# One completion count per copy for the token scatters of a routed layer on one core

## The chip, the cores and the metric

The kernel runs on one core of one Trainium2 chip. The metric is the device time of one execution in microseconds (us), the median of the runs given. The engines named below are PE (TensorE), DVE (VectorE), ACT (ScalarE), POOL (GpSimd) and SP (SyncE, which here issues DMAs only).

## The reference

The program computes two transformer-like layers on 16 sequences of 256 tokens with 128 features (4096 tokens). Layer 0 is a small state-space mixer and a mixture of 8 experts with 2 chosen per token. Layer 1 is a 16-head attention with relative positions and a second mixture of experts with hidden size 512. The change touches only that last part, which the reference writes densely:

```python
logits = relu(xf @ Wr1 + br1) @ Wr2 + br2
gates = softmax(logits); tg, ti = top_k(gates, 2); tg = softmax(tg / 2)
out = silu(xf @ Ws1 + bs1) @ Ws2 + bs2              # shared expert, all tokens
for e in range(8):
    h = silu(xf @ We1[e] + be1[e]) @ We2[e] + be2[e]
    w = sum(tg * (ti == e), axis=-1)
    out = out + w[:, None] * h
```

## The kernel before, in words

The kernel does not compute every expert for every token. It copies each token's feature row twice, once for each chosen expert, into a DRAM table `dispatched_rows` (`xsD` in the code) that has an area of 4096 rows for each expert. It then works through 39 tiles (`NG`) of 256 rows, each belonging to one expert, and scatters the results back to `expert_results` (`yD`).

**Routing.** Tokens are handled in 8 chunks of 512 (`NC`), and two chunks form one of 4 groups (`GROUPS`). A group holds 8 columns of 128 tokens (`GN` is 8). For group g, DVE chooses the two experts (`choose(g)`, L1392), PE forms prefix sums (`ranks(g)`, L1906), and DVE turns them into row numbers (`destinations(g)`, L1414). The last instruction for each copy k (0 or 1) is the cast at L1424, which adds 1 to the semaphore `s_dest`. The feature rows themselves lie in `ROWS[0]` and `ROWS[1]`.

**Scattering, the place of the change.** POOL runs the loop at L725 to L735. For each group g and each copy k it waits for `s_dest`, then issues 8 indirect DMAs (L733), one for each column of 128 tokens, 129 floats per row. Ahead of each eight, the first one excepted, it waits at L730 until all earlier scatters have landed: all DMAs add 16 to the one semaphore `s_disp`, and the value waited for is 16 times the number issued so far. In all there are 4 x 2 x 8 = 64 scatters. The eights are called g0k0, g0k1, g1k0 and so on to g3k1 below. Nothing else runs on POOL between the first of them and the first result scatter of the tiles (L741).

**Who waits for the scatters.** SP does, once. After the tables of tiles are ready it loads the weights of the first four tiles (`load_weights`, L602), then waits at L613 for `s_sdn` to reach 8 (PE has finished the shared expert for all 8 chunks, which frees memory that the tiles use), then at L614 for all 64 scatters, and then loads the rows of the first four tiles (`load_rows`: a register load at L595 and the DMA at L596).

**What PE and DVE do meanwhile.** PE runs the shared expert: `shared_up(c)` (L1930) and `shared_down(c)` (L1940), whose last matmul adds 1 to `s_sdn`. For each chunk DVE waits for that count, adds a bias (L1428), multiplies by a gate (L1027) and adds to the residual (L1030), which adds 1 to `s_res`. The orders of `shared_up`, `shared_down`, `project` and `ranks` on PE and of `shared_out`, `choose` and `destinations` on DVE are written out by hand. PE waits for `s_res` to reach 8 at L2026, and then for the rows of tile 0 (L1999); its first instruction of the tiles is the transpose at L2002. Then each tile goes through L2002, L2011 (up), L925 (ACT), L2021 (down), L1518 (DVE) and L741 (POOL).

Of the kernel before, what the change touches and what calls it, by code (L numbers as in the profile page):

```python
# [26 lines left out]
NT = TOK // P  # L27
# [39 lines left out]
GN = GC * TPC  # L67
# [6 lines left out]
def build(nc, A, out):  # L74
    ctx = ExitStack()
    with ctx:
# [3 lines left out]
        def sem(name):  # L80
            return ctx.enter_context(nc.semaphore(name))
# [169 lines left out]
        ROWS = [v.rearrange("p (t n) -> p t n", t=NT) for v in (rows0, R.take(NT * RW))]  # L251
# [117 lines left out]
        s_tot = sem("s_tot")  # L369
        s_rank = sem("s_rank")  # L370
        s_dest = sem("s_dest")
        s_disp = sem("s_disp")
        s_sup = sem("s_sup")
        s_sact = sem("s_sact")
        s_sdn = sem("s_sdn")
# [44 lines left out]
        def _(sp):  # L420
# [71 lines left out]
            for c in range(NC):  # L492
# [3 lines left out]
                k = c % 2  # L496
# [114 lines left out]
            for k in range(UT):  # L611
                load_weights(k, k)
            sp.wait_ge(s_sdn, NC)  # L613
            sp.wait_ge(s_disp, 16 * 2 * NT)  # L614
            for k in range(UT):
                load_rows(k, k)
            def next_tiles(i, n):
# [24 lines left out]
        def _(pool):  # L642
# [31 lines left out]
            for c in range(NC):  # L674
                k = c % 2
# [49 lines left out]
            for g in range(GROUPS):  # L725
                pool.wait_ge(s_ids, 1 + (g > 0))
                pool.wait_ge(s_rows, 2 * GC * (g + 1))
                for k in range(2):
                    if g or k:
                        pool.wait_ge(s_disp, 16 * GN * (2 * g + k))  # L730
                    pool.wait_ge(s_dest, 2 * g + k + 1)
                    for t in range(g * GN, (g + 1) * GN):
                        nc.gpsimd.indirect_dma_start(  # L733
                            xsD[:, :], bass.IndirectOffsetOnAxis(ap=dest[k][:, t:t + 1], axis=0),
                            ROWS[k][:, t, :], None).then_inc(s_disp, 16)  # L735

            def results_out(j, k):
                pool.wait_ge(s_ys, j + 1)
# [1420 lines left out]
```

## Time and profile before

| what | us |
|---|---|
| median of 3 runs | 982.03 |
| lowest and highest of the 3 | 975.97, 982.88 |
| the profiled execution, whole | 988.27 |
| its span from the first to the last instruction | 986.4 |
| its mean granted TensorE clock | 0.917 of full |

The span is what the trace covers. The profiled execution's own time has 1.87 us around it. It is one execution, and it is 6.24 us above the median of the three runs. In the rows below a line of the timeline or of the chain begins with the start in us from the span's start and the length in us; what stands in brackets is the time that the engine sat idle before it, and what ended that. "Issue" means that nothing which the profile shows ended it, and "remote" that the releaser was not found.

### The profile page before, as it was taken

To read this page: it belongs to the slowest core of one execution; us is meant where nothing else is said; L and a number is where in the kernel's file an instruction comes from. 1 tells how busy PE (TensorE), PEld (TensorE's weight loads), DVE (VectorE), ACT (ScalarE), POOL (GpSimd) and SP (SyncE) were. 2 spreads that over 40 slices of the span, in tenths; PEclk is the share of its full clock that TensorE was granted. 3 is DMA by queue.
4 is the path that set the end of the run, shared out by engine and by line. 5 is a ranking of instruction groups with operands and counts; after the bars stand their busy time and mean duration, and the time that the engine had idled before them with its cause. 6 is when DMAs were issued, how large, how long until landed. Compare 5 with 4: busy or idle time off the path is not lost.

```text
span 986.4 us, 22653 instructions
## 1 busy us (share of the span) xinstructions
PE 837.8 (85%) x8752; PEld 581.6 (59%) x8752; DVE 608.9 (62%) x1652; ACT 354.6 (36%) x670; POOL 246.8 (25%) x248
## 2 busy tenths in 40 slices
PE   3876498999994979999999999998789889999960
PEld 3665355666663544666565665654456678888850
DVE  8882767666687888777877877865346322222218
ACT  1403112122224120563463463563545334444424
POOL 1040000000043640001211211214465624444440
PEclk9985589999997975999999999999799989999985
DMA  8995000000003673214423413312131437777746
GB/s 236 316 321 193 0 2 15 9 9 8 8 0 120 180 215 95 57 27 107 100 32 100 100 28 94 67 30 67 34 84 39 140 100 209 212 220 211 215 126 220
DMA packets 108820, 107.17 MB, mean 109 GB/s; under 512 B 50029, under 2 KB 95022, under 8 KB 108046
## 3 DMA queue, kind: packets, MB, share of 16 engines
q1 hardware_dynamic: 104190, 96.63, 34.9%
q0 software_dynamic: 4544, 9.35, 2.7%
q8 instruction: 60, 0.98, 0.4%
q14 instruction: 26, 0.21, 0.1%
HBM read 80.97 MB, written 44.77 MB: 127 GB/s over the span
## 4 chain that ended last, share of the span: by engine, by line
PE 57%; DVE 19%; issue 10%; SPq 5%; DMA 4%; ACT 2%; POOL 2%; POOLq 0%; DVEq 0%; another core or an unknown queue 0%; ACTq 0%
PE bank L2011 7%; PE bank L1791 7%; PE bank L2021 6%; PE bank L1627 5%; PE bank L1638 5%; PE bank L1639 5%; DVE sb_arena L1259 5%; PE bank L1731 4%; PE bank L1683 4%; PE bank L1709 3%; DMA sb_arena<-in_iota 2%; DVE sb_arena L1249 2%; DVE sb_arena L1251 2%; PE bank L1612 1%; PE bank L1593 1%
## 5 line engine op out<-in xcount | busy, mean ns | idle before, releaser
L1259 DVE TRANSPOSE_TENSOR_REDUCE sb_arena<-bank 128x16 f32<-128x512 f32 x192 | 120.3, 685 | 23.2 <-PE bank L1731 21.8
L837 ACT ACTIVATE sb_arena<-bank 128x512 f32<-128x512 f32 x192 | 99.2, 602 | 50.0 <-PE bank L1731 50.0
L925 ACT ACTIVATE sb_arena<-bank,sb_arena 128x256 f32<-128x256 f32 x156 | 65.3, 471 | 101.7 <-PE bank L2011 100.9
L741 POOL DMA_INDIRECT expert_results<-sb_arena x78 | 74.9, 960 | 94.1 <-DVE sb_arena L1518 77.8
L1627 PEld LDWEIGHTS bank<-sb_arena 128*128 128x128 f32 x512 | 67.5, 194 | 46.5 <-issue 25.7
L794 ACT ACTIVATE sb_arena<-bank 128x512 f32<-128x512 f32 x64 | 38.2, 598 | 152.4 <-PE bank L1639 152.4
L2011 PE MATMUL bank<-sb_arena 128*128 128x256 f32 x312 | 78.7, 396 | 4.6 <-DVE sb_arena L1514 2.1
L1627 PE MATMUL bank<-sb_arena 128*128 128x128 f32 x512 | 69.6, 280 | 14.8 <-DVE sb_arena L1170 14.8
L1791 PE MATMUL bank<-sb_arena 128*16 128x128 f32 x1024 | 72.9, 421 | 5.1 <-issue 4.8
L1170 DVE TENSOR_TENSOR sb_arena<-sb_arena,bank 128x512 f32<-128x512 f32 x64 | 43.7, 685 | 52.7 <-ACT sb_arena L794 52.4
L2021 PE MATMUL bank<-sb_arena 128*128 128x128 f32 x624 | 75.9, 275 | 0.0
L733 POOL DMA_INDIRECT dispatched_rows<-sb_arena x64 | 63.5, 992 | 45.7 <-issue 18.9
L1152 DVE SCALAR_TENSOR_TENSOR sb_arena<-bank,sb_arena 128x128 f32<-128x128 f32 x256 | 71.7, 343 | 3.0 <-PE bank L1627 3.0
L2021 PEld LDWEIGHTS bank<-sb_arena 128*128 128x128 f32 x624 | 72.8, 192 | 0.1
L1638 PE MATMUL bank<-sb_arena 128*128 128x512 f32 x128 | 69.0, 622 | 0.0
L1639 PE MATMUL bank<-sb_arena 128*128 128x512 f32 x128 | 67.5, 609 | 0.0
L2011 PEld LDWEIGHTS bank<-sb_arena 128*128 128x128 f32 x312 | 57.2, 193 | 16.5 <-issue 7.5
L1683 PE MATMUL bank<-sb_arena 128*128 128x56 bf16 (+1 forms) x512 | 62.2, 281 | 5.4 <-DVE sb_arena L1239 3.1
L1249 DVE CAST sb_arena<-bank 128x512 bf16<-128x512 f32 x64 | 43.6, 682 | 37.0 <-PE bank L1683 37.0
L1512 DVE CAST sb_arena<-sb_arena 128x2 uint32<-128x2 f32 x39 | 7.3, 186 | 94.7 <-DMA expert_results<-sb_arena 78.4
L667 POOL TENSOR_TENSOR sb_TMP<-sb_arena,sb_GATE 128x256 f32<-128x256 f32 x16 | 11.3, 726 | 214.4 <-DVE sb_arena L1152 214.3
L1731 PE MATMUL bank<-sb_arena,sb_identb 128*32 128x128 bf16 (+1 forms) x2304 | 62.4, 241 | 0.4 <-DVE sb_arena L1249 0.4
(252 smaller groups left out, 1395.4 us busy)
## 6 DMA issues: line engine op xcount, KB each, us to landing
sb_arena<-in_w SPq DMA_DIRECT2D x39, 578.0 KB
dispatched_rows<-in_padding SPq DMA_DIRECT2D x8, 2064.0 KB, 34.6
sb_arena<-dispatched_rows SPq DMA_DIRECT2D x39, 129.0 KB
sb_GATE<-gates SPq DMA_DIRECT2D x2, 2048.0 KB, 7.0
sb_arena<-q_parts SPq DMA_DIRECT2D x8, 512.0 KB, 5.7
sb_arena<-k_parts SPq DMA_DIRECT2D x8, 512.0 KB, 6.8
context_rel<-sb_arena SPq DMA_DIRECT2D x256, 8.0 KB
sb_arena<-expert_results SPq DMA_DIRECT2D x16, 256.0 KB, 5.8
```

What stands on the lines that cost most here:

```text
L741: nc.gpsimd.indirect_dma_start(yD[:, :], bass.IndirectOffsetOnAxis(ap=rid[:, k, r:r + 1], axis=0), YS[:, k, r, :], None).then_inc(s_yo[k], 16)
L837: nc.scalar.activation(dst, src, ACT.Exp).then_inc(s_ex, 1)
L1152: ins = v.scalar_tensor_tensor(out=ACC[:, T, :], in0=src[:, t * D:(t + 1) * D], scalar=wstep[:, (j // NC) % 2, T:T + 1], in1=ACC[:, T, :], ...
L1259: v.tensor_reduce(dst.rearrange("p h b -> p (h b)"), bank[r % RING][:, :].rearrange("p (b c) -> p b c", c=32), AX, ALU.max, apply_transpos ...
L1627: ins = mm(bank[4 + j % 2][:, t * D:(t + 1) * D], HM0[:, j % 2, t * P:(t + 1) * P], W0[:, k, 2 * F0:3 * F0], start=True, stop=True)
L1638: mm(bank[j % 2][:, :], W0[:, k, 0:F0], chunk(hT, c), start=True, stop=True)
L1639: mm(bank[2 + j % 2][:, :], W0[:, k, F0:2 * F0], chunk(hT, c), start=True, stop=True).then_inc(s_up[0], 1)
L1683: ins = mm(out[:, :, :, x], GT4[:, first:first + 32, :].rearrange("p x a -> p (x a)"), queries[:, :, :, q], start=True, stop=True, skip_gr ...
L1731: ins = mm(dst[32 * b:32 * b + 32, :, 32 * b:32 * b + w], identb[:, 32 * a:32 * a + 32], src[:, :, :].rearrange("p (g b) q -> p g b q", g= ...
L1791: ins = mm(out[32 * j:32 * j + 2 * HD, :, x], relk[:, 32 * j + 8 * w + 2 * x:32 * j + 8 * w + 2 * x + 2, :], four, start=True, stop=True, ...
L2011: ins = mm(bank[2 * (k % 2) + b // 2][:, b % 2 * GT:(b % 2 + 1) * GT], W1[:, k, b * P:(b + 1) * P], XT[:, k % 2, :], start=True, stop=True ...
L2021: ins = mm(bank[6 + k % 2][:, r * D:(r + 1) * D], HMT[:, k % 2, b, r * P:(r + 1) * P], W1[:, k, I1 + b * D:I1 + (b + 1) * D], start=(b == ...
```

## The change

The semaphore `s_disp` becomes a pair, one for copy 0 and one for copy 1. Ahead of the eight of group g and copy k, POOL waits only until the eights of the same copy in the groups before g have landed, instead of until all scatters issued so far have landed. Group 0 waits for no landing at all. SP waits for both counts, each half as high, instead of for one.

```diff
-        s_disp = sem("s_disp")
+        s_disp = [sem(f"s_disp{k}") for k in range(2)]
@@ SP, ahead of the rows of the first four tiles
             sp.wait_ge(s_sdn, NC)
-            sp.wait_ge(s_disp, 16 * 2 * NT)
+            for k in range(2):
+                sp.wait_ge(s_disp[k], 16 * NT)
             for k in range(UT):
                 load_rows(k, k)
@@ POOL, the scatters
                 for k in range(2):
-                    if g or k:
-                        pool.wait_ge(s_disp, 16 * GN * (2 * g + k))
+                    if g:
+                        pool.wait_ge(s_disp[k], 16 * GN * g)
                     pool.wait_ge(s_dest, 2 * g + k + 1)
                     for t in range(g * GN, (g + 1) * GN):
                         nc.gpsimd.indirect_dma_start(
                             xsD[:, :], bass.IndirectOffsetOnAxis(ap=dest[k][:, t:t + 1], axis=0),
-                            ROWS[k][:, t, :], None).then_inc(s_disp, 16)
+                            ROWS[k][:, t, :], None).then_inc(s_disp[k], 16)
```

## Rows read from the trace of the kernel before

**Rows 1.** The page: the chain that ended last, its shares by engine.
```profile
PE 57%; DVE 19%; issue 10%; SPq 5%; DMA 4%; ACT 2%; POOL 2%; POOLq 0%; DVEq 0%; another core or an unknown queue 0%; ACTq 0%
```

**Rows 2.** The instructions of line 733, the scatters: a summary over the span.
```profile
L733 POOL DMA_INDIRECT dispatched_rows<-sb_arena x64: 955/962/1327, 680.6 to 786.4; - x64
...
  DMA dispatched_rows<-sb_arena: 9.0, 4
```

**Rows 3.** Timeline of POOL: first scatters of g0k1 to g3k1, and the last.
```profile
692.31 0.96 POOL L733 DMA_INDIRECT dispatched_rows<-sb_arena  x1 [1.67 <-DMA dispatched_rows<-sb_arena]
...
711.25 0.96 POOL L733 DMA_INDIRECT dispatched_rows<-sb_arena  x1 [9.12 <-DVE sb_arena L1424]
...
722.96 0.96 POOL L733 DMA_INDIRECT dispatched_rows<-sb_arena  x1 [1.81 <-issue]
...
735.30 0.96 POOL L733 DMA_INDIRECT dispatched_rows<-sb_arena  x1 [2.17 <-DMA dispatched_rows<-sb_arena]
...
747.58 0.96 POOL L733 DMA_INDIRECT dispatched_rows<-sb_arena  x1 [1.58 <-DMA dispatched_rows<-sb_arena]
...
763.72 0.96 POOL L733 DMA_INDIRECT dispatched_rows<-sb_arena  x1 [6.32 <-DVE sb_arena L1424]
...
777.30 1.23 POOL L733 DMA_INDIRECT dispatched_rows<-sb_arena  x1 [3.58 <-DMA dispatched_rows<-sb_arena]
...
786.43 0.96 POOL L733 DMA_INDIRECT dispatched_rows<-sb_arena  x1 [0.30 <-issue]
```

**Rows 4.** The chain of waits from 786 us on: start, length, what.
```profile
788.74 0.23 another core or an unknown queue
788.98 0.27 SPq L595
...
789.70 2.30 DMA sb_arena<-dispatched_rows
...
792.13 0.67 PE bank L2002 x2
...
793.38 3.78 PE bank L2011 x8
...
798.17 1.99 PE bank L2011 x8
```

**Rows 5.** Timeline of PE: ends of `shared_down(5)`, and of 6 and 7.
```profile
774.47 0.27 PE L1940 MATMUL bank<-sb_arena 128*128 128x128 f32 x1 [0.20 <-issue]
...
778.71 7.31 PE L1940 MATMUL bank<-sb_arena 128*128 128x128 f32 x64
```

**Rows 6.** Timeline of DVE: bias for chunks 5, 6, 7, and last residual sum.
```profile
775.49 0.69 DVE L1428 TENSOR_TENSOR sb_arena<-bank,sb_arena 128x512 f32<-128x512 f32 x1 [5.13 <-PE bank L1940]
...
782.48 0.69 DVE L1428 TENSOR_TENSOR sb_arena<-bank,sb_arena 128x512 f32<-128x512 f32 x1 [4.78 <-issue]
...
788.99 0.69 DVE L1428 TENSOR_TENSOR sb_arena<-bank,sb_arena 128x512 f32<-128x512 f32 x1 [4.29 <-remote]
...
790.50 0.69 DVE L1030 TENSOR_TENSOR sb_X<-sb_X,sb_TMP 128x512 f32<-128x512 f32 x1
```

**Rows 7.** Timeline of DVE: the row numbers of copy 1, groups 2 and 3.
```profile
730.81 0.17 DVE L1424 CAST sb_arena<-sb_arena 128x8 uint32<-128x8 f32 x1
...
763.51 0.17 DVE L1424 CAST sb_arena<-sb_arena 128x8 uint32<-128x8 f32 x1
```

**Rows 8.** Timeline of SP: the weight loads of the first four tiles.
```profile
769.44 6.26 SPq L602 DMA_DIRECT2D sb_arena<-in_w  x4
```

**Rows 9.** Two stretches: length, busy and (instructions) of PE, PEld, DVE, ACT, POOL; PEclk, DMA share, GB/s.
```profile
794.00:798.00 4.00, 3.59 (x10) 2.45 (x8) 0.38 (x2) 1.64 (x4) 0.00 (x0) 0.50 0.14 33
798.00:880.00 82.00, 80.00 (x527) 72.20 (x528) 19.14 (x61) 33.98 (x83) 36.89 (x39) 1.00 0.69 196
```

**Rows 10.** Timeline of ACT: two long gaps that end as an eight lands.
```profile
690.67 0.71 ACT L814 COPY sb_arena<-bank 128x512 f32<-128x512 f32 x1 [7.01 <-remote]
...
722.83 3.54 ACT L880 ACTIVATE sb_arena<-bank,sb_arena 128x512 f32<-128x512 f32 x5 [6.32 <-remote]
```

## The prediction

> **What bounds the kernel now.** I read the page first, for the chain that ended last: it is PE for 57% of the span and POOL for 2% [rows 1]. POOL is a helper, so a change on its queue pays only where somebody waits for a scatter. The second view is the list of the instructions of line 733. It shows 64 scatters of 0.96 us each between 680.6 and 786.4 us, and it attributes 9.0 us of idle time ahead of four of them to the landing of earlier ones [rows 2]. The third view, the timeline of POOL, puts those four in place and shows a fifth: g1k1 has 1.81 us ahead of it under the name "issue" [rows 3]. That is also the landing, since a scatter in the middle of an eight has only 0.30 us ahead of it, as the last line of that group shows [rows 3]. The fourth view is the chain from 786 us on. There the scatters do touch the path: SP's wait for them is over at 788.74, SP's register load starts at 788.98, the DMA of tile 0's rows at 789.70, and PE's first transpose of the tiles at 792.13 [rows 4]. The last two views are PE and DVE in the same stretch, since SP waits for `s_sdn` too [rows 5, 6].
>
> **What the change removes.** The wait at L730 today costs, over the 0.30 us that any scatter has ahead of it: 1.37 us for g0k1, 1.51 for g1k1, 1.87 for g2k0, 1.28 for g2k1 and 3.28 for g3k1 [rows 3], 9.31 us together. g1k0 and g3k0 had 9.12 and 6.32 us ahead of them that ended with DVE's row numbers, so what is gained before them is lost there.
>
> For g0k1: it starts 1.37 us earlier, and g1k0 still starts at 711.25. Nothing is left.
>
> For group 1 and group 2: g1k1 starts at 721.45 in place of 722.96. Its issuing ends at 735.30 - 2.17 = 733.13, so it takes 10.17 us, and is now done at 731.62. g2k0 needs then g1k0's landing, which is there by 722.96, and row numbers that are there at 730.98, when even copy 1's are finished [rows 7]. It starts at 731.92 in place of 735.30, issues for 747.58 - 1.58 - 735.30 = 10.70 us, and g2k1 starts at 742.92 in place of 747.58. That is 4.66 us sooner, and g3k0 still starts at 763.72, for its numbers come from DVE at about that time [rows 7]. All of it is swallowed. Nobody but POOL waits for the first 48 scatters.
>
> For group 3: g3k0 ends issuing at 777.30 - 3.58 = 773.72. Copy 1's numbers are there at 763.68 [rows 7], and g2k1 landed long before. So g3k1 starts at 774.02, 3.28 us sooner, and its last scatter ends at 787.39 - 3.28 = 784.11. Today the last one ends at 787.39 and its landing is seen at 788.74, 1.35 us later [rows 3, 4]. So the last landing comes at 785.46.
>
> **What it adds.** One more wait on SP with its count already full: today's step from the one wait to the register load, 0.23 us [rows 4], bounds a second one from above, and zero from below. I take 0.05. One semaphore more costs nothing in time. POOL has one wait fewer. No instruction on PE, DVE or ACT changes.
>
> More scatters are in flight at once. The weight loads of the first four tiles are issued from 769.44 to 775.70 [rows 8], and g3k1 now begins at 774.02, inside their traffic. The only row for scatters beside that traffic is g3k0: its landing took 3.58 us where the other eights took 1.58 to 2.17, so at most 2.0 us longer [rows 3]. I take zero, because the last of g3k1 is issued 8 us after the last weight load. With the 2.0 us the last landing is at 787.46, still before 788.74. A backlog cannot build up where POOL needs 1.26 us for each scatter and the data of an eight is in 1.3 to 1.9 us after its last one [rows 3, 4]. The weights themselves may come some tenths later, and the first tile needs them at 793.38 only.
>
> **What is late next.** SP's register load also needs `s_sdn` at 8, the end of `shared_down(7)`. PE's row ends at 786.02 [rows 5]. But DVE's bias for chunk 7, which waits for that count alone, starts at 788.99, after 4.29 us of idling, at the very moment at which SP goes on [rows 4, 6]. So in this execution the two things SP waits for came together, 0.24 us apart, and PE's count came 2.97 us after the end of PE's row. For chunk 5 the same distance is 774.74 to 775.49, 0.75 us. For chunk 6 it is about nothing: half of the 64 matmuls that end at 786.02 are chunk 6's, so it ends near 782.4, and DVE starts at 782.48 [rows 5, 6].
>
> How late the count of chunk 7 is in the runs that are timed decides everything. From below it is 0.0 us (chunk 6), from above 2.97 (this execution). I take 0.75, the row of chunk 5, which lies nearest in traffic and in what PE does. Then SP goes on at 786.02 + 0.75 + 0.05 = 786.82 instead of 788.98. The rows of tile 0 take 792.13 - 788.98 = 3.15 us from there, so PE starts the tiles at 789.97 and not at 792.13. DVE's last residual sum, which PE also needs, follows its bias by 791.19 - 788.99 = 2.20 us and would be at 788.97, out of the way [rows 6]. The gain is 2.16 us. From then on every tile hangs on the one before, with PE busy 80 of 82 us [rows 9], and I see nothing that would give it back.
>
> The Trainium skill, in "Perfetto Trace Analysis" (the section on the Tensor Engine instruction), says that the end of a matmul in a profile is estimated from its size, and that the semaphore follows when PSUM has taken the data. By that rule 786.02 is no measured end and 788.99 is the real one in every run, and the sum would be a gain of zero. The rows of chunks 5 and 6 speak for a short distance, that of chunk 7 for the long one; it is the first rival below.
>
> **The sum.** The span of 986.4 us goes to 984.2, and the profiled execution from 988.27 to 986.1. The median of the runs lies 6.24 us under that execution. I take the difference over unchanged: 982.03 - 2.16 = 979.9 us.
>
> **Rivals.**
>
> First, `s_sdn` is as late as in the trace in every run. SP goes on at 788.98 whatever the scatters do, and the gain is 0 to 0.1 us: 982.0. For it speaks that DVE and SP are let go within 0.01 us of each other [rows 4, 6]. Against it: the rows of the two chunks before.
>
> Second, the start of the tiles moves and the clock with it. PE was idle for 6.11 us ahead of 792.13, and then had a granted clock of 0.50, the 1.2 GHz level, from 794 to 798; the first eight matmul rows of L2011 took 3.78 us and the next ones 1.99 [rows 4, 5, 9]. With the start at 789.97 the idle time is 3.95 us. If the clock then stays at 2.4 GHz, 1.8 us more are saved, and somewhat more with the transposes beside them: 982.03 - 2.16 - 1.8 = 978.1. Against it: the idle time is still long.
>
> Third, slower. ACT was let go after 7.01 us of idling at 690.67, just as g0k0 had been issued to the end (692.31 - 1.67 = 690.64), and after 6.32 us at 722.83, between the end of g1k0 at 721.15 and the start of g1k1 at 722.96; both times it waited for PE [rows 3, 10]. The release at 788.99 came 0.25 us after the last landing. If a running train of scatters holds up PE's counts until it has drained, then the pauses at L730 are what lets them through, and the change removes them. g0k0 and g0k1 would become one train from 680.63 to 692.31 - 1.37 + 10.1 = 701.0 (eight times 1.26 us), and ACT's copy at 690.67 would move to 701.0. That copy stands ahead of the last pair's context, on which the shared expert's end hangs, and so up to 10.4 us pass on: 982.03 + 10.4 = 992.4, and with the later gain kept 990.3. It decides from the point where ACT's copy is held over 2.2 us longer than now. Against it: DVE's bias at 782.48 was let go in the middle of g3k1, 0.1 us after PE had finished [rows 6], so a train does not hold up every count.
>
> Fourth, the change doesn't do what it says: POOL stops on its own with 16 scatters in flight, at the same places and for as long. 982.0. The trace has never more than eight in flight, so no row excludes it.
>
> **How the numbers follow.** Forecast, a gain of 1 to 3 us: 0.43. First rival: 0.33. Second: 0.08. Third: 0.12, of which 0.05 for more than 9.8 us and the rest for 1 to 9 us slower. Fourth: 0.04. The three runs before spread from 975.97 to 982.88, so a difference of under 1%, 9.8 us, is about what a measurement of this kernel can't tell from no change. Forecast, first, second and fourth rival lie within it. I leave 0.04 for a gain over 1%, for which no mechanism is in the rows beyond the spread of the runs. Slower by over 1% has 0.05, and no change has 0.91. The range: the low end is the forecast less the 6.06 us by which the fastest run lay under the median, 973.8, and the high end is the first rival's 982.0 and 3.5 us of the third one's smaller part, 985.5.
>
> **What would show it.** In the timeline of POOL, 0.30 us ahead of g0k1 and g2k1, g2k0 at about 732, g3k1 at about 774.0 and the last scatter's end at about 784.1. g1k0 and g3k0 should still start within a microsecond of DVE's casts. In the chain, SP's register load should start right with DVE's bias for chunk 7, since the scatters are no longer last. If that bias starts at 786.8 the forecast holds, and at 789.0 the first rival. The second shows as a granted clock of 1.00 after the tiles have started. The third shows as an ACT copy (L814) that starts at about 701 instead of 690.67. The prediction is wrong if g3k1 starts later than about 775, or if the last landing is still what SP waits for.

## The result, and the profile after

| | before | changed |
|---|---|---|
| median, us | 980.48 (4 runs) | 968.40 (4 runs) |
| lowest and highest | 975.97, 982.88 | 967.30, 970.52 |
| the profiled execution, whole | 988.27 | 970.52 |
| its span | 986.4 | 968.7 |

The ratio is 0.9895 [0.9863, 0.9926] (in brackets the 95% interval), a gain of 10 us by the ratio and of 12 by the medians. The ratios of this document leave out executions more than 1.5% above the fastest of the same kernel, and they are not the quotient of the medians, from which they differ by up to half a percent. The forecast was 979.9 with 973.8 as the low end. Which chip these runs met is not on record. On chip B (below) the result came again, and on two others the same kernel is 1.6 and 2.3% slower than before.

The summary of the scatter line (734 in the changed kernel) answers to [rows 2]:

```profile
L734 POOL DMA_INDIRECT dispatched_rows<-sb_arena x64: 953/959/1450, 684.8 to 768.9; - x64
its engine sat idle before it (us, times) until:
  issue: 17.7, 58
  DVE sb_arena L1425: 5.5, 3
...
  DMA dispatched_rows<-sb_arena: 0.6, 2
```

The timeline of POOL in the changed kernel, first scatters of g0k1 to g3k1 and the last one, answers to [rows 3]:

```profile
695.12 0.96 POOL L734 DMA_INDIRECT dispatched_rows<-sb_arena  x1 [0.30 <-issue]
...
705.28 0.96 POOL L734 DMA_INDIRECT dispatched_rows<-sb_arena  x1 [0.30 <-issue]
...
715.39 0.96 POOL L734 DMA_INDIRECT dispatched_rows<-sb_arena  x1 [0.30 <-issue]
...
726.26 0.96 POOL L734 DMA_INDIRECT dispatched_rows<-sb_arena  x1 [0.30 <-issue]
...
736.81 1.15 POOL L734 DMA_INDIRECT dispatched_rows<-sb_arena  x1 [0.30 <-issue]
...
749.56 0.95 POOL L734 DMA_INDIRECT dispatched_rows<-sb_arena  x1 [2.75 <-DVE sb_arena L1425]
759.94 0.96 POOL L734 DMA_INDIRECT dispatched_rows<-sb_arena  x1 [0.30 <-issue]
...
768.86 1.45 POOL L734 DMA_INDIRECT dispatched_rows<-sb_arena  x1 [0.30 <-issue]
```

The landing waits are gone: the 0.6 us that are left of 9.0 are two times the 0.30 us that any scatter has ahead of it. But see g1k0 at 705.28. It has 0.30 us ahead of it, where before it waited 9.12 us for DVE. POOL now issues 48 scatters without a stop. The casts of DVE are ready earlier, 717.25 and 749.35 against 730.81 and 763.51 in [rows 7]. These are copy 1's of groups 1, 2 and 3 in its timeline:

```profile
702.29 0.17 DVE L1425 CAST sb_arena<-sb_arena 128x8 uint32<-128x8 f32 x1
...
717.25 0.34 DVE L1425 CAST sb_arena<-sb_arena 128x8 uint32<-128x8 f32 x1
...
749.35 0.17 DVE L1425 CAST sb_arena<-sb_arena 128x8 uint32<-128x8 f32 x1
```

The chain of waits of the changed kernel at the start of the tiles answers to [rows 4]:

```profile
768.86 2.77 DMA dispatched_rows<-sb_arena
771.64 0.03 SPq L615
771.67 0.04 issue
771.71 0.27 SPq L595
...
772.43 2.16 DMA sb_arena<-dispatched_rows
774.60 0.14 issue
774.73 0.57 PE bank L2003 x2
```

Now the last landing, at 771.63, is what SP waits for. PE and DVE at the end of the shared expert, timelines, answer to [rows 5, 6]:

```profile
763.83 6.97 PE L1941 MATMUL bank<-sb_arena 128*128 128x128 f32 x61
...
770.84 0.69 DVE L1429 TENSOR_TENSOR sb_arena<-bank,sb_arena 128x512 f32<-128x512 f32 x1 [1.36 <-PE bank L1941]
```

PE ends at 770.80 and DVE goes on at 770.84. The 2.97 us between the two in the trace before are 0.04 us here.

### The profile page after: what moved, and what is told of

Read it like the earlier page. It is cut to its first block, busy times and chain, and to the rows that moved or that the text cites. A ratio compares the mean times of both kernels' runs of the same rounds, so it can differ in the third digit from the quotient of the medians.

```text
span 968.7 us, 22652 instructions
## 1 busy us (share of the span) xinstructions
PE 833.2 (86%) x8752; PEld 581.0 (60%) x8752; DVE 610.3 (63%) x1652; ACT 354.9 (37%) x670; POOL 246.8 (25%) x248
## 4 chain that ended last, share of the span: by engine, by line
PE 59%; DVE 20%; DMA 8%; issue 4%; POOL 4%; ACT 2%; SPq 2%; POOLq 0%; DVEq 0%
PE bank L1792 7%; PE bank L2012 6%; PE bank L1628 5%; PE bank L2022 5%; PE bank L1639 5%; PE bank L1640 5%; PE bank L1732 4%; PE bank L1684 4%; DVE sb_arena L1260 3%; DMA expert_results<-sb_arena 3%; PE bank L1710 3%; DMA sb_arena<-in_iota 2%; DVE sb_ST L960 2%; PE bank L1764 2%; DVE sb_arena L1250 2%
## 5 line engine op out<-in xcount | busy, mean ns | idle before, releaser
L1260 DVE TRANSPOSE_TENSOR_REDUCE sb_arena<-bank 128x16 f32<-128x512 f32 x192 | 120.3, 685 | 24.3 <-PE bank L1732 23.2
L1628 PEld LDWEIGHTS bank<-sb_arena 128*128 128x128 f32 x512 | 67.3, 194 | 47.4 <-issue 25.4
L1792 PE MATMUL bank<-sb_arena 128*16 128x128 f32 x1024 | 68.0, 423 | 0.0
L1639 PE MATMUL bank<-sb_arena 128*128 128x512 f32 x128 | 67.4, 609 | 0.0
L1640 PE MATMUL bank<-sb_arena 128*128 128x512 f32 x128 | 66.5, 602 | 0.0
```

What stands on the lines that cost most here:

```text
L1260: v.tensor_reduce(dst.rearrange("p h b -> p (h b)"), bank[r % RING][:, :].rearrange("p (b c) -> p b c", c=32), AX, ALU.max, apply_transpos ...
L1628: ins = mm(bank[4 + j % 2][:, t * D:(t + 1) * D], HM0[:, j % 2, t * P:(t + 1) * P], W0[:, k, 2 * F0:3 * F0], start=True, stop=True)
L1639: mm(bank[j % 2][:, :], W0[:, k, 0:F0], chunk(hT, c), start=True, stop=True)
L1640: mm(bank[2 + j % 2][:, :], W0[:, k, F0:2 * F0], chunk(hT, c), start=True, stop=True).then_inc(s_up[0], 1)
L1792: ins = mm(out[32 * j:32 * j + 2 * HD, :, x], relk[:, 32 * j + 8 * w + 2 * x:32 * j + 8 * w + 2 * x + 2, :], four, start=True, stop=True, ...
```

## The experiments

They ran in batches. All kernels of a batch ran on one chip, and each ratio is against the kernel before on that chip. The batches met five chips, called A to E. The median of the kernel before was 1002.6 and 1004.6 us on A (two batches), 982.2 on B, 1002.7 on C, 995.2 on D and 977.3 on E. In the first four expectations theory A puts the gain down to the waiting taken away, theory B to the counts and their numbering.

### Chip A, the change taken apart

**e1**: two counts, but waiting as before (against the changed kernel).

```diff
                     if g:
                         pool.wait_ge(s_disp[k], 16 * GN * g)
+                    if g or k:
+                        pool.wait_ge(s_disp[1 - k], 16 * GN * (g + k))
```

> The two counts of the changed kernel, but POOL waits ahead of each eight for all earlier scatters, as the kernel before does. Theory A, what is gained comes from the removed waiting (POOL's pauses hold up PE's counts to ACT and DVE, or PE itself): as slow as before, 980 us or ratio 0.997 to 1.003. Theory B, the gain comes from the counts themselves (one semaphore that takes 16 increments from each of two eights, or the semaphores and instructions behind it being numbered and placed otherwise): ratio about 0.989, as the changed kernel.

998.44 us, ratio 0.9972 [0.9922, 1.0022]. Two counts alone do nothing here that can be told from no change.

**e2**: no landing wait on POOL (against the kernel before).

```diff
-                    if g or k:
-                        pool.wait_ge(s_disp, 16 * GN * (2 * g + k))
```

> The kernel before with one count, and no waiting for landings on POOL at all (line 730 gone); SP still waits for all 64. Theory A: as fast as the changed kernel or slightly faster, ratio 0.985 to 0.990. Theory B: ratio 0.997 at most, the 2 us of the forecast. If many scatters in flight hold up others, slower than the changed kernel, above 0.992.

1025.64 us, ratio 1.0242 [1.0167, 1.0316]: slower, although it takes away more waiting than the change does.

**e3** leaves out the wait ahead of g0k1 (`if g:` in place of `if g or k:`), **e4** the one ahead of g3k1 (`if (g or k) and (g, k) != (3, 1):`).

> The kernel before without the wait ahead of g0k1 alone. In the trace before, PE's matmuls of L1791 stuttered from 690 to 704 us, from the moment at which POOL reached that wait. Theory A: that stutter is gone, and most of the gain is here: ratio 0.989 to 0.993. My forecast's steps, by which this wait is hidden: 1.000.

> The kernel before without the wait ahead of g3k1 alone. By the forecast's steps all that can be gained is here, 0 to 3 us: ratio 0.997 to 1.000. Theory A says the same for this one, since nothing but the end of the shared expert lies beside it. Theory B: 1.000.

e3: 1004.33 us, ratio 0.997 [0.9928, 1.0012], so no change, and the stutter of PE that was to go with this wait is still in its trace (29.2 us in column 1 of the table at the end of this section). e4: 1007.75 us, 1.0092 [1.0054, 1.0131]. The wait ahead of g3k1 is the one that my prediction counted on, and the kernel without it is slower here, by 0.5 to 1.3%. The trace of e4 does not show how: its g3k0, which comes ahead of the missing wait, already starts 4.9 us later than e1's, counted from the first scatter.

### Chip B, both kernels again

> The changed kernel once more, beside the kernel before on one chip, since the four kernels above all had a long stretch (34 to 36 us) from the first scatter to the first matmul of the shared expert, where the changed kernel's trace has 21.6 us. If the gain is the change's own, the ratio is 0.985 to 0.993 and that stretch is 20 to 24 us. If it was luck or the chip of that run, the ratio is 0.995 to 1.005 and the stretch 34 to 36 us.

> The kernel before, as if it were changed, to see how far its own repeats spread and what its trace looks like on this chip. All theories: ratio 1.000 within its interval; the stretch from the first scatter to the first shared matmul 34 to 36 us, with PE's matmuls of L1791 in small bursts while scatters are in flight.

Changed (e5): 968.41 us, ratio 0.9873 [0.9802, 0.9944]. Before (e6): 979.76 us, 0.9976 [0.9946, 1.0006]. The gain is back. In both traces PE gets from the first scatter to the shared expert in 22.2 us. For the kernel before I had expected 34 to 36, as on A, so on this chip something that held PE up on A is missing. The timeline of POOL in e6, the kernel before, is the one that I should have had:

```profile
696.50 0.95 POOL L733 DMA_INDIRECT dispatched_rows<-sb_arena  x1 [1.58 <-DMA dispatched_rows<-sb_arena]
...
708.69 0.96 POOL L733 DMA_INDIRECT dispatched_rows<-sb_arena  x1 [2.39 <-DMA dispatched_rows<-sb_arena]
...
721.84 0.96 POOL L733 DMA_INDIRECT dispatched_rows<-sb_arena  x1 [3.35 <-DMA dispatched_rows<-sb_arena]
...
758.36 0.95 POOL L733 DMA_INDIRECT dispatched_rows<-sb_arena  x1 [2.48 <-DMA dispatched_rows<-sb_arena]
...
770.36 0.96 POOL L733 DMA_INDIRECT dispatched_rows<-sb_arena  x1 [1.73 <-DMA dispatched_rows<-sb_arena]
...
779.51 0.96 POOL L733 DMA_INDIRECT dispatched_rows<-sb_arena  x1 [0.30 <-issue]
```

All seven gaps end with a landing, none with DVE. DVE casts the numbers of g1k1 at 703.08 in this trace, and the eight that uses them starts at 721.84. POOL's scatters are one chain, and it ends the wait of SP (the chain of waits of e6):

```profile
779.51 2.28 DMA dispatched_rows<-sb_arena
781.82 0.04 issue
781.86 0.27 SPq L595
```

PE's shared expert has been over since 772.34, so here the scatters bound the start of the tiles, and a landing wait that goes should come back in full.

### Chip A again, the changed kernel and pauses that wait for nothing

A train is a run of scatters with only 0.30 us between them. The train theory of the expectations is that POOL's scatters bound the start of the tiles, so that each gap between them counts. The stall theory is that PE, or the counts that it sends, stop while a long train runs.

**e7** is the changed kernel, **e9** e2's kernel, **e10** e1's. **e8** is the changed kernel with pauses:

```diff
                     if g:
                         pool.wait_ge(s_disp[k], 16 * GN * g)
+                    if g or k:
+                        for _ in range(3):
+                            wait(pool, s_pause, n_pause)
+                            nc.gpsimd.memset(PAUSE[:, :], 0.0).then_inc(s_pause, 1)
+                            n_pause += 1
```

> The changed kernel once more, beside the kernel before, on whichever chip this batch meets. Train theory: once DVE's row numbers are in time, POOL has nothing to do but issue scatters from the first to the last, each landing wait at L730 pushes all later scatters back by its 1.3 to 3 us, and the tiles start when the last scatter has landed; the gain is then 8 to 11 us, a ratio of 0.988 to 0.992, wherever PE runs without stalls. Stall theory: on a chip where PE and its counts stall about 10 us into a running train of scatters, the longer trains of the changed kernel cost more than the waits did: ratio 1.00 to 1.02, with PE idle by 5 to 10 us in the middle of the stretch from 690 to 790.

> The changed kernel with a pause of three small memsets on POOL (1.5 to 1.9 us together, estimated from 3.5 us for 128x4096) ahead of each eight except the first, waiting for nothing. Train theory: seven pauses lie in a train that is bound by POOL, so the last scatter ends 8 to 13 us later than in the changed kernel and the time is that of the kernel before within 3 us, although no landing is waited for. Stall theory: the pauses, not the landings, are what lets PE through; on a chip that stalls this kernel is as fast as the kernel before, and faster than the changed one by the stalls. A theory in which the landing itself matters (counts, numbering, fewer waits) expects the time of the changed kernel plus at most 2 us.

> POOL waits for no landing at all; SP waits for all 64 at the one count. Train theory: the waits that the changed kernel keeps cost it nothing (its gaps are 0.3 us), so this is the time of the changed kernel within 2 us, where PE does not stall. Stall theory: as on the chip of its first run, 2 to 3 per cent slower than the kernel before, and slower than the changed kernel by up to 1 per cent, since its trains run to 16 scatters the same way.

> Two counts as in the changed kernel, but each eight waits for all earlier scatters through both of them, so the waiting is that of the kernel before. Train theory and stall theory alike: the time of the kernel before within 3 us, ratio 0.997 to 1.003. A theory in which the numbering or the number of counts gives the gain expects 0.988.

| | us | ratio |
|---|---|---|
| e7 changed | 1023.48 | 1.0162 [1.0082, 1.0242] |
| e8 changed, pauses | 995.91 | 0.988 [0.9794, 0.9967] |
| e9 no landing waits | 1020.94 | 1.0171 [1.0108, 1.0235] |
| e10 two counts, waits as before | 995.68 | 0.9896 [0.9832, 0.996] |

The changed kernel is slower on this chip, and seven pauses of 1.9 us make it 27.6 us faster. e10 lies lower than expected (e1, the same kernel, had 0.9972). The two intervals overlap only from 0.9922 to 0.996, so I read no gain into it; it is a reason not to trust a fraction of a percent from one batch, and some tenths of a percent from the second count are not excluded. e10 and e7 differ in one thing, the wait for the other copy's scatters, and without it the kernel is 27.8 us slower: so it is the missing waiting that costs here. e9 against e7 shows no cost of the waits which the changed kernel keeps. The timeline of PE in e7, after the first scatter at 684.02, shows where the time goes:

```profile
692.11 1.38 PE L1792 MATMUL bank<-sb_arena 128*16 128x128 f32 x17
694.04 1.13 PE L1792 MATMUL bank<-sb_arena 128*16 128x128 f32 x4 [0.55 <-issue]
...
697.64 0.38 PE L1792 MATMUL bank<-sb_arena 128*16 128x128 f32 x1 [1.04 <-issue]
699.06 0.37 PE L1792 MATMUL bank<-sb_arena 128*16 128x128 f32 x1 [1.04 <-issue]
...
704.74 0.38 PE L1792 MATMUL bank<-sb_arena 128*16 128x128 f32 x1 [1.75 <-issue]
```

Matmuls that by the profile wait for nothing come one at a time, 0.7 to 2.1 us apart, until shortly after POOL's train of 16 ends at 704.1. These 64 matmuls take from 692.11 to 709.40. In the changed kernel of the first result they are one row, of 4.17 us. Later in e7 it is worse. These are rows of PE, DVE, ACT and POOL from its timelines, in that order:

```profile
752.36 3.74 PE L1941 MATMUL bank<-sb_arena 128*128 128x128 f32 x32
755.93 3.60 PE L1931 MATMUL bank<-sb_arena 128*128 128x512 f32 x8
...
766.49 0.69 DVE L1429 TENSOR_TENSOR sb_arena<-bank,sb_arena 128x512 f32<-128x512 f32 x1 [11.07 <-remote]
...
768.64 1.28 ACT L881 ACT_TABLE_LOAD   x1 [12.89 <-remote]
...
765.75 0.96 POOL L734 DMA_INDIRECT dispatched_rows<-sb_arena  x1 [0.30 <-issue]
791.41 0.96 POOL L734 DMA_INDIRECT dispatched_rows<-sb_arena  x1 [24.71 <-DVE sb_arena L1425]
```

DVE waits for the matmuls of L1941 whose row ends at 756.10 and is let go at 766.49. ACT waits for those of L1931, whose row ends at 759.53, and goes on at 768.64. In between neither PE, DVE nor ACT does anything. POOL meanwhile issues the last of g2k0 and all of g2k1, up to 766.71. So PE stops, or its counts don't come through, while a train runs, and both come back as it ends. The row numbers of group 3 come late for it, and POOL then waits 24.71 us for them.

One rival can be looked up: that the engines ran out of instructions, whose transfers the scatters held up. These are all DMA packets of e7 from 759.5 to 766.5:

```profile
DMA packets 192, 0.40 MB, mean 57 GB/s; under 512 B 96, under 2 KB 96, under 8 KB 192
...
q0 software_dynamic: 192, 0.40, 17.5%
```

They are those of the scatters. No packet of an instruction queue is among them, and none comes from 766 to 773 either, where the engines go on, so nothing speaks for this rival. Nor are the scatters denser than elsewhere: e5, which has no such gap, has 188 of these packets and 17.3% from 720 to 727.

### Chip C, what ends the stall

**e13** and **e14** are the changed kernel and the kernel before. **e11** is e8 with `range(1)`, one memset a pause. **e12** has shorter trains (against the kernel before):

```diff
                     for t in range(g * GN, (g + 1) * GN):
+                        if t % 8 == 4:
+                            pool.wait_ge(s_disp, 16 * (GN * (2 * g + k) + 4))
```

> As the changed kernel with pauses, but only one memset (about 0.6 us) ahead of each eight except the first, too short for the 1.3 to 1.6 us in which the last scatter lands. Stall theory in the form that a train has to drain before PE gets through: the pause does not help, and on a chip that stalls the time is that of the changed kernel plus up to 3 us. Stall theory in the form that POOL has to stop issuing for a moment: it helps most of the way, the time is within 5 us of the kernel with three memsets. Where PE does not stall: the changed kernel plus 4 us (seven times 0.6).

> The kernel before with one landing wait more in the middle of each eight, so that no train is longer than four scatters, some 5 us of issuing. Stall theory: PE stalls only from about 10 us of a running train on, so no stall is left; on a chip that stalls this kernel is 8 to 20 us faster than the kernel before, although POOL waits eight times more. Train theory, where PE does not stall: eight waits of 1.4 us in a train bound by POOL, 8 to 12 us slower than the kernel before.

> The changed kernel on the chip of this batch. Where PE does not stall: ratio 0.987 to 0.990. Where it stalls: 1.015 to 1.02, with DVE idle for 10 us or more before a bias of the shared expert (L1429) that waits for PE.

> The kernel before on the chip of this batch, for its profile. Ratio 0.997 to 1.003. Where PE does not stall: eights in POOL's timeline 1.3 to 3.4 us apart and the tiles at about 785. Where it stalls: gaps of 6 to 9 us before g1k0 and g3k0, the last L1791 at 711 to 714, and the tiles from 795 on.

| | us | ratio |
|---|---|---|
| e11 short pauses | 1014.02 | 1.0135 [1.0081, 1.0189] |
| e12 landed every four | 994.49 | 0.9917 [0.9884, 0.9949] |
| e13 changed | 1022.81 | 1.0227 [1.0167, 1.0288] |
| e14 before | 1000.49 | 0.9965 [0.9918, 1.0013] |

e12 waits 15 times where the kernel before waits 7 times, and is faster. Its POOL timeline, and that of PE in the stretch in which e7 was in pieces:

```profile
687.09 0.96 POOL L735 DMA_INDIRECT dispatched_rows<-sb_arena  x1 [1.59 <-DMA dispatched_rows<-sb_arena]
...
693.58 0.95 POOL L735 DMA_INDIRECT dispatched_rows<-sb_arena  x1 [1.64 <-DMA dispatched_rows<-sb_arena]
```

```profile
688.17 4.27 PE L1793 MATMUL bank<-sb_arena 128*16 128x128 f32 x56
692.79 0.72 PE L1793 MATMUL bank<-sb_arena 128*16 128x128 f32 x8 [0.35 <-issue]
```

The same stretch in e14, the kernel before on the same chip, begins like this, and it goes on in such pieces up to 707.47:

```profile
690.85 1.65 PE L1791 MATMUL bank<-sb_arena 128*16 128x128 f32 x16
693.32 1.10 PE L1791 MATMUL bank<-sb_arena 128*16 128x128 f32 x4 [0.83 <-issue]
...
700.63 0.39 PE L1791 MATMUL bank<-sb_arena 128*16 128x128 f32 x1 [0.34 <-issue]
```

With trains of four the stall is all but gone, and with it the late count. In e14 the row of PE's last L1940 ends at 786.92 and DVE's bias for it starts 5.16 us later, just after POOL's last train (timeline of DVE):

```profile
792.08 0.69 DVE L1428 TENSOR_TENSOR sb_arena<-bank,sb_arena 128x512 f32<-128x512 f32 x1 [6.48 <-remote]
```

In e12 PE's last L1940 ends at 772.98, 13.9 us earlier, and its count is 0.04 us late. But then POOL is the bound, with its last scatter over at 790.5, and most of PE's gain ends in a wait. That PE stalled only from about 10 us of a train on, the premise of e12's expectation, holds no better than roughly: in e14 the matmuls come in pieces from 693.3 on, 10.0 us after the first scatter, but again in the second train from 699.2 on, after 4.3 us. e11, pauses of 0.7 us, is 8.8 us faster than e13 by the medians, where I expected either 3 us slower or nearly e8. The two intervals overlap, and the fastest run of e13, 1011.61, lies below all four of e11, so that a pause shorter than a landing helps is not shown. That it does less than one of 1.9 us (27.6 us on chip A) is, as far as chips can be compared.

### Chips D and E, the mix

**e16** is e12's kernel, **e17** e8's. **e15** and **e18** have the trains of four in groups 0 and 1 only (`if t % 8 == 4 and g < 2:`).

> Trains of four with a landing wait between them in groups 0 and 1, where PE stalled most and POOL waits for DVE anyway; trains of eight with all landings waited for, as in the kernel before, in groups 2 and 3. On a chip where PE stalls: four waits of 1.4 us fewer than with fours everywhere, so the last scatter ends near 785 to 787 and the time is 3 to 5 us under that kernel, 10 to 13 us under the kernel before; if PE stalls anew in the last two groups, 5 us of that are lost. Where PE doesn't stall: 4 to 6 us slower than the kernel before.

> Trains of four everywhere, as in e12. Where PE stalls: 0.99 again, with the shared expert's last matmul near 773. Where PE doesn't stall: POOL's train is the bound in both kernels, so eight more waits of 1.4 us make it 8 to 12 us slower than the kernel before, ratio 1.008 to 1.012.

> The changed kernel with seven pauses of 1.6 us that wait for nothing. Where PE stalls: 0.988 again, against a changed kernel at 1.016 to 1.023. Where PE doesn't stall: the train of POOL is longer than the changed kernel's by seven times 1.6 us less what lay beside waits for DVE, 8 to 11 us; the time is the kernel before's within 3 us, which means that POOL's train and nothing in the landings is what the changed kernel shortened.

> The kernel of e15 once more, on the chip that the batch meets. Where PE stalls: ratio 0.985 to 0.995 against the kernel before. Where it doesn't: 4 to 6 us slower than the kernel before, ratio 1.004 to 1.006, since POOL's train is the bound there and has four waits of 1.4 us more.

| | chip | us | ratio |
|---|---|---|---|
| e15 four in two groups | D | 986.35 | 0.9914 [0.9875, 0.9953] |
| e16 landed every four | D | 994.11 | 0.9996 [0.9961, 1.0031] |
| e17 changed, pauses | D | 990.92 | 0.9952 [0.991, 0.9994] |
| e18 four in two groups | E | 983.59 | 1.0075 [1.004, 1.0109] |

On D e16 and e17 gain less than on C and A, and e16 met neither of its two expectations: the kernel before is 7.5 us faster on D than on C, while e16 has the time of e12. e15 is 8.9 us faster than the kernel before on D, where I had expected 10 to 13, and 7.8 faster than e16, where I had expected 3 to 5. The same kernel is 6.3 us slower on E, where I had expected 4 to 6. That is what the train theory gives on a chip without the stall: PE ends at 765.6 there and POOL at 784.5. The summary of the scatters in e18 has the extra waits:

```profile
L735 POOL DMA_INDIRECT dispatched_rows<-sb_arena x64: 952/958/1349, 679.5 to 783.6; - x64
...
  DMA dispatched_rows<-sb_arena: 26.0, 11
```

### All profiled executions side by side

e1 and e10, e2 and e9, e12 and e16, e8 and e17, e15 and e18 are pairs of the same kernel. Worked out from the timelines: (1) from the first scatter to the end of the last L1791, (2) from the first L1930 to the end of the last L1940, (3) from there to DVE's last bias, which waits for it, (4) the idle time between the 64 scatters, (5) from the first scatter to the first transpose of the tiles. All in us; lines by the kernel before.

| | 1 | 2 | 3 | 4 | 5 |
|---|---|---|---|---|---|
| before, as predicted from | 27.8 | 70.8 | 2.97 | 43.3 | 111.5 |
| changed, first result | 15.3 | 64.4 | 0.04 | 21.7 | 89.9 |
| B e6 before | 16.0 | 65.2 | 0.04 | 32.5 | 100.0 |
| B e5 changed | 15.9 | 63.2 | 0.04 | 21.5 | 89.5 |
| A e1 two counts, waits as before | 29.1 | 70.7 | 4.75 | 47.0 | 114.4 |
| A e2 no landing waits | 29.5 | 99.3 | 0.04 | 62.5 | 138.2 |
| A e3 first wait gone | 29.2 | 82.8 | 2.51 | 56.7 | 124.1 |
| A e4 last wait gone | 29.3 | 83.8 | 0.04 | 47.2 | 122.9 |
| A e10 two counts, waits as before | 28.0 | 70.7 | 3.98 | 45.2 | 113.0 |
| A e7 changed | 29.6 | 104.2 | 0.04 | 65.2 | 143.2 |
| A e8 changed, pauses | 25.7 | 81.3 | 1.57 | 49.1 | 117.4 |
| A e9 no landing waits | 28.8 | 102.4 | 0.04 | 64.0 | 140.6 |
| C e14 before | 29.1 | 68.2 | 5.16 | 44.0 | 111.9 |
| C e13 changed | 29.0 | 98.0 | 0.04 | 57.0 | 136.5 |
| C e11 changed, short pauses | 29.6 | 91.0 | 0.04 | 54.8 | 129.8 |
| C e12 landed every four | 16.7 | 65.9 | 0.04 | 47.4 | 114.5 |
| D e15 four in two groups | 16.4 | 69.8 | 0.04 | 37.1 | 105.0 |
| D e16 landed every four | 16.9 | 63.0 | 0.05 | 44.5 | 111.6 |
| D e17 changed, pauses | 24.3 | 77.5 | 1.66 | 46.0 | 114.3 |
| E e18 four in two groups | 15.4 | 64.4 | 0.04 | 41.8 | 109.5 |

In e8 and e17 column 3 is no late count: DVE was busy with the chunk before, for whose count it had waited over 9 us. The profiled execution of e8 was the slowest of its four, 1001.16 us. Column 1 has two levels, 15 to 17 and 24 to 30. On B, and in the changed kernel's first result, it is low. On A and C, with e17 on D, and in the execution of before that I predicted from, it is high, unless the trains are four long. e18's low value is no evidence on E, since its trains there are four long; that E has no stall is read from column 2, 64.4 with trains of eight in groups 2 and 3, and from the median of the kernel before, 977.3 us. On B column 4 falls by 11.0 and column 5 by 10.5, which is the change's own gain. On C the changed kernel loses 29.8 in column 2.

## Why the prediction was wrong

**The step that failed** is "what is gained before them is lost there", about g1k0 and g3k0, and with it "All of it is swallowed." Both rows that carried it, 9.12 and 6.32 us of waiting for DVE [rows 3], are rows of a stalled execution. The [rows 3, 7] of a quiet one are those of e6: the casts for group 1 come at 702.29 and 703.08, over 5 us before POOL gets to g1k0 at 708.69, POOL waits for landings only, and the seven waits add up. The idle time between scatters shrinks by 11.0 us there (column 4). I had priced 9.31 us for the five waits, kept 3.28 of them, and let the wait for `s_sdn` take a third of that. The sign of the forecast was right on chip B and in the first result, but it hung on 2 us that are not where the gain came from, and it was wrong on A and C.

**What I had in hand.** The profiled execution was 988.27 us, above all three timed runs, the highest of which was 982.88. I named this distance and subtracted over it, as if 6.24 us were spread evenly. Rows 10 show two of its stalls, which I used only for a rival. Whether that execution ran on the chip of the timed runs is not on record. If it did, the stall comes and goes on one chip.

**g3k1 and the last landing.** I had the last scatter at 784.11 and the landing 1.35 us behind. The landing distance is right: the last scatter ends at 770.31 and has landed at 771.63, 1.32 us later. The place is 13.8 us off, of which the swallowed waits are one part and the missing stall the other.

**What is late next.** I expected `s_sdn` to be SP's last wait, 0.75 us late. Without a stall it is 0.04 us late, and the scatters are SP's last wait in both kernels (e6: 781.82 against 772.38). So the forecast's 2.16 us and the first rival's zero both rested on a wait that is not there. The Trainium skill says in "Perfetto Trace Analysis" (the section on the Tensor Engine instruction) that the end of a matmul is estimated, and that its semaphore is updated once PSUM has acknowledged the writes. No trace contradicts that, but the page gives no distance, and "in every run" was my own addition. The distance is no constant of the kernel. It is 0.04 us wherever the shared expert ends without a stall, with a train running (e6, e15, e18) or without, and 2.51 to 5.16 in the five stalled executions whose last matmuls end within the train of g3k1 (before, e1, e3, e10, e14).

**The added wait of SP.** Priced at 0.05. From the landing to the register load it is 0.08 us in the changed kernel (771.63 to 771.71), and 0.07 in e6 (781.79 to 781.86), so about nothing.

**Second rival, the clock.** PE was idle for 3.93 us before the tiles, as I had worked out (3.95), and the granted clock was at the 1.2 GHz level all the same when the tiles had started: 0.50 from 776 to 784. The rival falls. Stretches of the changed kernel, columns as in [rows 9]:

```profile
776.00:780.00 4.00, 4.00 (x10) 2.85 (x10) 0.00 (x0) 1.16 (x3) 0.00 (x0) 0.50 0.25 62
780.00:784.00 4.00, 3.41 (x9) 2.71 (x9) 0.49 (x2) 1.37 (x4) 0.00 (x0) 0.50 0.00 0
```

**Third rival, slower.** Its mechanism is real, and its upper price, 10.4 us, was too low: 18.9 us on A and 20.1 on C in the medians. The row that I held against it, DVE let go in the middle of g3k1 [rows 6], shows only that a stall does not hold every count. In the changed kernel's profiled execution of the first result it did not appear.

**Fourth rival.** POOL does not stop by itself: up to 48 scatters were issued at 0.30 us distance.

**The 0.04 for a gain over 1%, "for which no mechanism is in the rows",** was the chance that I had set too low. The chances of the five cases already add up to 1.00 without it. The mechanism was the ordinary one, the waits themselves, had they not been hidden. On a chip with no stall the sum is plain: seven waits, in e6's trace 15.4 us by 7 landings, less the 0.30 us each that any scatter has, less the 2.2 us more for which g3k0 then waits for DVE (2.54 us ahead of it in e5). That is 11.1, for 11.0 us in column 4 and 10.5 in column 5. The medians moved by 12.1 and 13.8, and by 11.4 against e6's own ten runs. By the intervals of the ratios the gain is 7.3 to 13.4 us in the first result and 5.5 to 19.4 on B, so the 11 us of the waits lie inside, and there is nothing on top that the runs could tell from noise. The two profiled spans of chip B differ by 8.4 us. That the kernel before had a stall in some of its timed runs there is not shown.

**What stays open:** why PE stalls while scatters are issued, and why on chips A and C and, by its median and e17's 24.3 us in column 1, on D, but not on B and, so far as its rows tell, on E. The experiments show that the length of an unbroken train decides (e7 against e10 and e8 on A, e12 against e14 on C), and that the two counts are not what costs. A landing wait is not needed for the break: those that e8 keeps are over before it gets to them. But its pauses of 1.9 us are also longer than the 1.3 us of a landing, so whether the stop of POOL or the landing frees PE is open; e11, made to separate the two, is not clear of noise. They don't show what PE lacks. Nothing was tried that separates the issuing on POOL from the traffic of the scatters. On a chip without the stall the waits themselves were varied only in the changed kernel and in e18.

## What to carry to other kernels

Ask of every wait that a profile shows as hidden whether what hides it is a fixed cost or a disturbance of that one execution. A profiled execution slower than all timed runs is a warning, and the cover that it shows should be priced at zero as one end of the range. Measure a change that packs DMAs of POOL closer on more than one chip: here the same edit was worth 1.3% one way and 2.3% the other. Where both kinds of chip must be served, short trains where PE is the bound and long ones where POOL is (e15) gained 0.9% on D and lost 0.7% on E. No kernel that was run on both kinds of chip beats the kernel before on both; e8, e10 and e12 were never run on B or E.

## What the hardware showed that I had not expected

- On three of five chips PE's matmuls came one or two at a time, 0.7 to 2.1 us apart, while POOL issued scatters of 128 rows each 1.26 us. 64 matmuls that take 4.2 us in the first result took 17.3 us in e7.
- All three compute engines stood still for some 7 us (759.5 to 766.5 in e7) with POOL alone going on, and went on as the train ended.
- A pause of POOL that waits for nothing, seven times 1.9 us, made the kernel 27.6 us faster on A. Seven of 0.7 us gave 8.8 us on C by the medians, which is not clear of noise.
- The last scatter of a train lands 1.3 us after it has been issued. The wait for it costs 1.6 to 3.4 us in e6, in which the scatter's 0.30 us is contained. It was 5.32 us in e12 (ahead of 766.65), where the four weight loads had just been issued, from 757.78 to 762.14.
